# An attention and pooling kernel on one core: head pairs interleaved in the columns of q and k, and the first two batches' score rows sent from SBUF to SBUF

## The reference, cut to what matters

```
query = side + b_self;   q = query @ Wq + bq
k     = (x + b_prev) @ Wk + bk          # keys of the batch's own 256 tokens
k_s   = query @ Wk + bk                 # one more key for each query: its own
v, v_s likewise from x and side, without the biases b_prev, b_self
score = softmax([q.k / 4 with keys >= seq_len masked,  (q * k_s).sum / 4])
x     = x + (score @ [v, v_s]) @ Wo + bo
# second layer
s = tanh(x @ W1 + b1) @ v1;  p = softmax(s under one of three masks, by kind)
out = x + (p @ x) / count
```

## Time and profile before

| | before |
|---|---|
| median of 3 runs | 281.02 us (279.83 to 283.24) |
| profiled execution | 281.62 us |
| its span, first to last instruction | 279.9 us |
| busy: PE / DVE / ACT / POOL | 238.4 / 184.4 / 156.6 / 76.3 us |
| chain that ended last: PE / DVE / DMA / issue | 59 / 13 / 9 / 8 % of the span |
| mean granted TensorE clock | 0.95 of full speed |
| DMA traffic | 35.50 MB in 28021 packets, 24416 of them under 2 KB |

### The profile page before, as it was taken

The page is one execution under the profiler, slowest core; times in us unless marked ns, Lnnn a source line. Parts: engine busy times, 40 slices in busy tenths (PEclk is TensorE's granted clock), DMA queues, the critical chain, the costliest instruction groups (busy, mean ns, idle before and its releaser), DMA issues.

```text
span 279.9 us, 6089 instructions
## 1 busy us (share of the span) xinstructions
PE 238.4 (85%) x2100; PEld 187.4 (67%) x2100; DVE 184.4 (66%) x384; ACT 156.6 (56%) x297; POOL 76.3 (27%) x87
## 2 busy tenths in 40 slices
PE   2986898599979999999999989999999769886732
PEld 2984787367758777877788768777787455563622
DVE  2659655457469758875887588758985885335631
ACT  4351223376477557755785667557856546772430
POOL 8026011013025103610451035103511330316111
PEclk9999669599999999999999999999999997999977
DMA  5469636913865096609560946096409410011011
GB/s 152 103 235 233 138 112 182 210 31 115 242 142 188 5 248 134 228 16 252 119 227 20 256 108 225 18 246 118 150 33 261 95 72 2 8 34 37 0 40 37
DMA packets 28021, 35.50 MB, mean 127 GB/s; under 512 B 4440, under 2 KB 24416, under 8 KB 28000
## 3 DMA queue, kind: packets, MB, share of 16 engines
q1 hardware_dynamic: 27360, 33.12, 44.6%
q0 software_dynamic: 640, 2.10, 2.0%
HBM read 20.26 MB, written 14.69 MB: 125 GB/s over the span
## 4 chain that ended last, share of the span: by engine, by line
PE 59%; DVE 13%; DMA 9%; issue 8%; ACT 5%; SPq 3%; POOL 1%; ACTq 0%; DVEq 0%; POOLq 0%
PE ps_any L1080 20%; PE ps_any L1134 10%; PE ps_max L1108 9%; PE ps_any L1087 6%; DMA k_rows<-k_spill 5%; PE ps_exp L1121 4%; DVE s_max L887 4%; DMA k_spill<-k_lo 3%; PE ps_any L1184 3%; PE ps_any L1240 2%; DVE bv_cast L854 2%; SPq L418 1%; ACT pt L623 1%; PE ps_any L1200 1%; PE ps_any L1166 1%
## 5 line engine op out<-in xcount | busy, mean ns | idle before, releaser
L887 DVE TENSOR_REDUCE s_max<-ps_max 128x4 f32<-128x1024 f32 x64 | 78.1, 1220 | 25.1 <-PE ps_max L1108 25.1
L623 ACT ACTIVATE pt<-ps_exp 128x1024 f32<-128x1024 f32 x64 | 65.6, 1025 | 50.1 <-PE ps_exp L1121 49.5
L1108 PE MATMUL ps_max<-k_rows,q_rows 49*128 49x256 f32 x256 | 33.7, 343 | 13.0 <-DMA k_rows<-k_spill 7.2
L1108 PEld LDWEIGHTS ps_max<-k_rows,q_rows 49*128 49x128 f32 x256 | 20.2, 194 | 24.6 <-DVE s_max L887 10.4
L1134 PE MATMUL ps_any<-pt,v_aug 128*32 128x256 f32 x512 | 36.0, 401 | 0.0
L1121 PE MATMUL ps_exp<-q_rows,k_rows 51*128 51x256 f32 x256 | 27.0, 288 | 2.3 <-ACT pt L623 2.3
L578 POOL TENSOR_TENSOR attn<-num,rden 128x256 f32<-128x256 f32 x16 | 9.6, 621 | 54.0 <-DVE rden L1030 54.0
L1121 PEld LDWEIGHTS ps_exp<-q_rows,k_rows 51*128 51x128 f32 x256 | 20.3, 191 | 4.1 <-ACT pt L623 2.7
L569 POOL TENSOR_TENSOR prod_lo<-prod,prod_hi 128x512 fp32r<-128x512 f32 x8 | 10.3, 1282 | 42.2 <-ACT prod_hi L714 42.2
L1080 PE MATMUL ps_any<-st_hi,w_hi 128*128 128x256 f32 x64 | 20.9, 326 | 0.3 <-DVE st_lo L912 0.3
L1134 PEld LDWEIGHTS ps_any<-pt,v_aug 128*32 128x32 f32 x512 | 13.7, 112 | 10.5 <-issue 1.3
(11 more groups left out here) (145 smaller groups left out, 605.3 us busy)
## 6 DMA issues: line engine op xcount, KB each, us to landing
q_rows<-q_spill SPq DMA_DIRECT2D x32, 192.0 KB, 4.4
k_rows<-k_spill SPq DMA_DIRECT2D x32, 192.0 KB
q_spill<-q_hi SPq DMA_DIRECT2D x16, 256.0 KB, 2.5
k_spill<-k_hi SPq DMA_DIRECT2D x16, 256.0 KB, 2.5
s_sb<-in_fside_BxSxS SPq DMA_DIRECT2D x8, 256.0 KB, 3.7
x_sb<-in_x SPq DMA_DIRECT2D x8, 256.0 KB, 3.2
q_spill<-q_lo SPq DMA_DIRECT2D x8, 256.0 KB, 2.2
k_spill<-k_lo SPq DMA_DIRECT2D x8, 256.0 KB, 3.1
```

What stands on the lines that cost most here:

```text
L623: nc.scalar.activation(pt[:, 2 * j % 8:2 * j % 8 + 2], ps_exp[:], ACT.Exp).then_inc(p_ready, 1)
L887: nc.vector.tensor_reduce(s_max[:, j // MJ, :, :, j % MJ].rearrange("p t e -> p e t"), ps_max[:], AX.X, ALU.max).then_inc(max_found, 1)
L1108: last = pe.matmul(ps_max[:, e, t], q_rows[par][rows, j, P * t:P * t + P], k_rows[par][rows, j, :], start=True, stop=True)
```

## The change

The 256 columns of q and of k are dealt out in another order. Before, block 0 held the first heads of all pairs and block 1 the second ones. Now the first 64 partitions of both blocks hold the first heads and the last 64 the second ones, and the two blocks hold alternate pairs. So 64 partitions by two blocks are, read in order, 16 partitions by 8 pairs, which is the order of the score rows.

With that, the rows of batches 0 and 1 are sent straight from SBUF to SBUF (`direct`): 12 DMAs of 128 KB per batch, each from 64 partitions to 16, in 2 KB pieces; SP issues them, but for the four of k_hi of batch 0, which ACT issues. TensorE's wait at j = 0 is then for all rows of q and k (both halves). Batches 2 to 7 still go through DRAM, with both blocks of a partition side by side there, so that a spill is 128 pieces of 2 KB (before: 256 of 1 KB), and a placing is as large as before. The loads of batch 1 come behind batch 0's rows on SP, no longer before them.

The set-up changes too: bq and bk are loaded by four DMAs (before two); POOL sets the second buffer's ones ahead of its first other work (before: at the end of period -1); ACT's split of Wo moves behind `prod_hi`; in period -1 DVE computes k_lo before the product q * k_s; the output bias (`bias_out`) is added in period 0; the sum over a head's dimensions (`headsum`) and the copy of the own-key scores follow the new order.

```diff
-        q_spill = nc.dram_tensor("q_spill", [2, 3, P, S], F32).ap()
-        k_spill = nc.dram_tensor("k_spill", [2, 3, P, S], F32).ap()
...
+        q_spill = nc.dram_tensor("q_spill", [3, P, 2, S], F32).ap()
+        k_spill = nc.dram_tensor("k_spill", [3, P, 2, S], F32).ap()
...
+        def direct(queue, part, rows, sixteens, sent):
+            for c in sixteens:
+                for e in range(2):
+                    queue.dma_start(rows[64 * e + DH * c:64 * e + DH * c + DH].bitcast(F32),
+                                    part[P // 2 * e:P // 2 * e + P // 2].rearrange("p m t -> p (m t)").bitcast(F32)
+                                    ).then_inc(sent, 16)
+
+        def parts_free(engine, i, k, spilled, direct_sent, sent_per):
+
+            if isinstance(i, int) and 0 < 2 * i + k < 3:
+                engine.wait_ge(direct_sent, sent_per * (2 * i + k))
+            elif (n := count(i, k, 48, -96)) is not None:
+                engine.wait_ge(spilled, n)
...
-                if (n := held(count(i, k, placed_per, 0))) is not None:
+                if (n := held(count(i, k, placed_per, -2 * placed_per))) is not None:
...
-                            sp.dma_start(dram[:, c].rearrange("e p t -> p e t"), parts[part][:].bitcast(F32)
-                                         ).then_inc(spilled, 16)
+                            sp.dma_start(dram[c], parts[part][:].bitcast(F32)).then_inc(spilled, 16)
...
                     sp.dma_start(rows[64 * e:64 * e + ROWS, MJ * g:MJ * g + MJ].bitcast(F32),
-                                 dram[e].rearrange("c (d j) t -> (c d) j t", d=DH)[:, MJ * g:MJ * g + MJ]
+                                 dram.rearrange("c (e d g l) m t -> e g c d (l m t)", e=2, g=NM, l=2)[e, g]
...
+            def direct_q(i, k):
+
+                if i * 2 + k == 0:
+                    sp.wait_ge(rows_one, 2)
+                sp.wait_ge(q_copied, count(i, k, 1, 1))
+                direct(sp, q_hi, q_rows[k % 2], (0, 1), q_direct)
+                sp.wait_ge(q_lo_done, count(i, k, 1, 1))
+                direct(sp, q_lo, q_rows[k % 2], (2,), q_direct)
...
+            def direct_k(i, k):
+
+                if i * 2 + k > 0:
+                    sp.wait_ge(k_hi_done, count(i, k, 1, 1))
+                    direct(sp, k_hi, k_rows[k % 2], (0, 2), k_direct)
+                else:
+                    sp.wait_ge(masks_stored, 16)
+                mask = row(mask_dram, i, k).unsqueeze(0).unsqueeze(0).broadcast_to([2, NJ, S])
+                sp.dma_start(k_rows[k % 2][R_MASK:R_MASK + 65:64].bitcast(F32), mask).then_inc(k_direct, 16)
+                sp.wait_ge(k_lo_done, count(i, k, 1, 1))
+                direct(sp, k_lo, k_rows[k % 2], (1,), k_direct)
...
-                if isinstance(i, int) and 2 * i + k < 2:
+                if isinstance(i, int) and 0 <= 2 * i + k < 2:
                     load(i, k + 2)
...
+                if isinstance(i, int) and 2 * i + k < 1:
+                    direct_q(*nxt)
+                    if live(*b):
+                        place_max(*b, 0)
+                    direct_k(*nxt)
+                    if not live(*b):
+                        load(i, k + 2)
+                    if live(*prv) and not last:
+                        load_again(*prv)
+                    return
...
-                        elif g == 0:
-                            sp.wait_ge(rows_one, par + 1)
...
-                        if g == 0 and isinstance(i, int):
-                            sp.wait_ge(masks_stored, 16)
...
-                    sp.dma_start(bqk_raw[:, n, :], vec.rearrange("(j e d) -> d j e", e=2, d=DH)
-                                 ).then_inc(bias_loaded, 16)
+                    for m in range(2):
+                        sp.dma_start(bqk_raw[:, n, m:m + 1],
+                                     vec.rearrange("(j m f) -> m f j", m=2, j=MJ)[m].unsqueeze(2)
+                                     ).then_inc(bias_loaded, 16)
...
+            ones_rows(1)
...
+                parts_free(pool, i, k, spilled, q_direct, 96)
...
-                if first:
-                    ones_rows(1)
...
-                        dst = dst.rearrange("p (e d j) -> p e d j", e=2, d=DH)
-                        src = src.rearrange("p (j e d) -> p e d j", e=2, d=DH)
+                        dst = dst.rearrange("p (m f j) -> p m f j", m=2, j=MJ)
+                        src = src.rearrange("p (j m f) -> p m f j", m=2, j=MJ)
...
-                            act.wait_ge(k_spilled, n)
+                        parts_free(act, *c, k_spilled, k_direct, 112)
...
                         if first:
-                            weight_hi(3)
+                            act.wait_ge(rows_one, 2)
+                            act.wait_ge(k_hi_done, 1)
+                            direct(act, k_hi, k_rows[0], (0, 2), k_direct)
...
+                        if first:
+                            weight_hi(3)
...
-                        nc.scalar.activation(s_self[:, c[1] % 2].rearrange("p g t e j -> p (g t e j)"),
-                                             ps_any[:, bank_of("SS", *c), 0, 0:2 * H], ACT.Copy
+                        nc.scalar.activation(
+                            s_self[:, c[1] % 2].rearrange("p g t e (l m) -> p (g t) (e l) m", m=2),
+                            ps_any[:, bank_of("SS", *c), 0, 0:2 * H].rearrange("p (b m x) -> p b x m", m=2, x=4), ACT.Copy
...
-                    act.wait_ge(q_spilled, n)
+                parts_free(act, i, k, q_spilled, q_direct, 96)
...
-                dve.wait_ge(bias_loaded, 4 * 16)
+                dve.wait_ge(bias_loaded, 6 * 16)
...
+            def k_low(i, k):
+
+                dve.wait_ge(k_hi_done, count(i, k, 1, 1))
+                parts_free(dve, i, k, k_spilled, k_direct, 112)
+                for m in range(2):
+                    last = nc.vector.scalar_tensor_tensor(
+                        out=k_lo[:, m], in0=ps_any[:, bank_of("K", i, k), m],
+                        scalar=bqk_col[:, 1, m:m + 1], in1=k_hi[:, m].bitcast(F32),
+                        op0=ALU.add, op1=ALU.subtract)
+                last.then_inc(k_lo_done, 1)
...
                         setup_pooling()
+                    if isinstance(i, int) and (2 * i + k, s) == (0, 2):
                         dve.wait_ge(bv_product_ready, 1)
                         nc.vector.tensor_tensor(bias_out[:], bo_wide[:], ps_exp[:, 0, 0], ALU.add
                                                 ).then_inc(bias_out_done, 1)
...
+                            for g in range(NM):
+                                last = nc.vector.tensor_reduce(
+                                    headsum[:, MJ * g:MJ * g + MJ].rearrange("p (e l) -> p e l", e=2),
+                                    ident[:].rearrange("p (e d g l) -> p g e l d", e=2, g=NM, l=2)[:, g],
+                                    AX.X, ALU.max)
+                            last.then_inc(headsum_ready, 1)
...
+                        if first:
+                            k_low(*c)
+                            product(*c)
+                        else:
+                            product(*c)
+                            k_low(*c)
...
                 if j % MJ == 0:
-                    pe.wait_ge(q_placed[j // MJ], count(i, k, 32, 32))
-                    pe.wait_ge(k_placed[j // MJ], count(i, k, 48, 48))
+                    if isinstance(i, int) and 2 * i + k < 2:
+                        pe.wait_ge(q_direct, 96 * (2 * i + k + 1))
+                        pe.wait_ge(k_direct, 112 * (2 * i + k + 1))
+                    else:
+                        pe.wait_ge(q_placed[j // MJ], count(i, k, 32, -32))
+                        pe.wait_ge(k_placed[j // MJ], count(i, k, 48, -48))
...
-                by_block = bank[:, 0, 0:2 * H].rearrange("p (g t e j) -> p t e g j", g=NM, t=KB, e=2)
+                by_block = bank[:, 0, 0:2 * H].rearrange("p (g t m x) -> p t m g x", g=NM, t=KB, m=2)
                 for t in range(KB):
-                    for e in range(2):
+                    for m in range(2):
                         for part in (prod_hi, prod_lo):
-                            last = pe.matmul(by_block[:, t, e], part[:, e, P * t:P * t + P], headsum[:],
+                            last = pe.matmul(by_block[:, t, m], part[:, m, P * t:P * t + P], headsum[:],
```

45 lines of the change are left out of this document (16 added, 29 removed).

## The result

The changed kernel takes **367.84 us** (median of 4 runs, 364.14 to 369.5) against 282.13 for the kernel before on the same chip (4 runs, 279.83 to 285.58): a ratio of 1.306, 95% interval 1.289 to 1.322. It is 30% slower. The prediction was 277.6 in a range of 270 to 285.5. The profiled execution took 366.49 us (span 364.8), 84.9 more than the one before.

A forecast was written before the change was run, and what follows sets the result against it. TensorE was taken to bound itself from period 2 on, with all gains in the first 80 us. Terms 0.9 - 2.4 - 1.5 - 0.4 = -3.4 took 281.62 to 278.2; the median, 0.6 lower, was 277.6, range 270 to 285.5.

The forecast's parts named there:

- slower: Whole kernel: a time above 286.6 us, the worse half of rival B, direct DMAs over 1.32 us each; chance 0.09.
- Term 4: Batch 2's 2.12 us wait: spills ahead of it may run faster with 2 KB pieces; -0.4 us (0 to -1.15).
- Term 1: Start to batch 1's transposes: set-up, direct rows and the load behind them move these from 28.61 to 29.5; +0.9 us.
- The hold: Set-up: POOL's memsets hold DVE's small bias operations to 10.8, so the bias products come 2.1 us late.
- rival B: Direct rows starved by their 16 partitions, 1.26 us per DMA: slower by 4.6 us, a median of 285.6; chance 0.20.
- Term 2: Batch 1's rows: six direct DMAs are there at 49.9 instead of 52.35; -2.4 us (bounds -3.15 and 0).
- Term 3: Clock behind batch 1's wait: the half-clock stretch goes if that wait shrinks to 0.7; -1.5 us (bounds 0 and -4.7).
- Rival C: Nothing won: the start is held as long as the waits shrink; 281 us, within 1.5; chance 0.12.

The follow-up runs named there:

- pad_before: The kernel before with each third of the spilled rows starting 8 DRAM rows further on, so a placing's source no longer merges; 374.49 us, ratio 1.337.
- mended: The changed kernel with DRAM ordered feature, part, pair: spills are one DMA of 128 partitions, a placing's slowest dimension is 16; 280.8 us, ratio 0.996.
- split_before: The kernel before with each of a batch's six spills sent as two DMAs of 64 partitions instead of one of 128; 305.05 us, ratio 1.081.
- two_queues: mended with the direct DMAs of batch 0's high q parts shared between SyncE's queue and ScalarE's, by partition halves; 280.72 us, no ratio given.
- roundtrip: merged with batches 0 and 1 also sent through DRAM and batch 1's loads ahead of the rows again; 303.95 us, ratio 1.083.
- merged: The changed kernel with partition halves outermost in DRAM: a placing reads 48 even rows, a spill is two DMAs of 64 partitions; 305.48 us, ratio 1.086.

## Why the prediction was wrong, step by step

**The step that failed** is the sentence "From period 2 on TensorE bounds itself, and the change leaves that work as it is", with "Later batches wait 0.4 in all" behind it. The bytes and the number of placings stayed, the form of one did not. Its source went from a dimension of 48 rows to 3 by 16, and with that, by the share of 0.19, from 16 DMA engines to 3. I had taken that a placing costs as before because it has as many bytes and rows. `pad_before` alone is 94 us slower. `mended` wins the loss back. Nearly all of the miss is here: 78.7 of the 84.9 us lie behind 63.61, where only rows that go through DRAM are still to come. That a spill has to stay whole as well, I learned from `split_before`. The 0.09 that I gave to "slower" was for direct DMAs of over 1.32 us; they took 1.1 to 1.2, so the 30% does not bear it out. Term 4, for the longer pieces, is not seen: the wait of batch 2 in `mended` is 1.99, against 2.12.

**Term 1** (+0.9 forecast; +7.4 in the trace: batch 1's transposes start at 36.02, not 28.61). The hold came nearly as forecast (2.57 us, products 1.7 late and not 2.1). A direct DMA was mis-sized: 131 thousand bytes at the measured 112 to 121 GB/s are 1.1 to 1.2 us, not 0.84. That is above the 0.97 from which rival B decides, and B's first score at 32.1 was nearer to the 34.10 measured than the forecast's 27.9. B had counted ten of the twelve DMA times; all twelve stood in one line, 19.1 + 12 x 1.17 + 0.4 = 33.5. That is the line which the Trainium skill (DMA: Bandwidth & Descriptors, "Issuing engines are not separate DMA queues") speaks of, and for neighbouring partitions the trace agrees: from 21 us on the rate stays near 120 with ScalarE's DMAs still under way. In `two_queues`, with spread partitions, more than the issue time was won. The Trainium skill's table (SBUF — State Buffer, "Door 1: The DMA port swizzle") has 104 GB/s for 16 neighbouring partitions; the trace is above it by 14% (119 GB/s from 21 to 33 us). I had the rule in hand and gave it 0.20. Batch 1's side input came behind the rows, at 36.02 with a wait of 1.13, as described.

**Term 2** (-2.4). Batch 1 waited 4.72, not less than 3.15: six DMAs issued from 47.94 had landed by 58.5. In `mended`, with rows over 46 partitions, the wait for rows is gone: the mechanism was right, the rate decided it.

**Term 3** (-1.5). The sentence behind it, that both slow stretches follow idle time, does not carry over. In the changed kernel TensorE is at half clock from 26 to 29.3 us, ahead of its wait for batch 0's rows and without a gap. In `mended` it is at half clock from 46 to 54, and that begins before batch 1's first score at 51.78, while TensorE is busy; in `two_queues` the same stretch runs at full clock (us, busy (count), granted clock, DMA share, GB/s; in this order):

```profile
26.00:29.30 3.30, 3.30 (x13) 0.50 1.05 113
```

```profile
46.00:54.00 8.00, 7.01 (x47) 0.50 0.38 123
```

```profile
46.00:54.00 8.00, 5.89 (x62) 1.00 0.32 104
```

So that stretch did not hang on the wait for rows, and the term has no ground; what it hangs on is open. Where the waits were long, in batches 2 to 7 of the changed kernel, the clock was low behind each of them, and no term had that. The other way, the slow stretch behind batch 0's rows was shorter than before: 0.50 from 30 to 40 us there, full clock again from 40 on now, six microseconds behind the first score. From batch 1's transposes to its wait for rows TensorE needed 17.8 us (20.6 before). So its delay of 7.4 us at those transposes was 6.2 at batch 2's, although the wait between them was 1.6 longer.

**The sum without the failed step.** `mended` is the nearest to it: the change with whole spills and placings at the old rate, though with faster direct rows. It gave 0.996 (0.989 to 1.003). The forecast, 277.6 of 281.02, is 0.988, just below that interval, so the forecast gain of 3.4 us is not shown even there. Nor do its pieces fit: a faster rate than in the changed kernel made term 2, and term 3 is missing.

**Rival C**, nothing won (281 within 1.5, or 0.995 to 1.005), describes `mended` better than the forecast does, and I had given it 0.12. That the direct rows decide little is also what `roundtrip` against `merged` shows.

## What to carry to other kernels

When a DRAM layout changes, write down for each DMA that reads or writes it the dimensions that are left after merging, on both sides: the slowest one decides how many DMA engines work, and 3 by 16 is another DMA than 48 with the same bytes. In a trace the sign is a low, flat DMA share (0.19 is three of sixteen) under a long queue, with waits on unrelated loads behind it. When two forms of a spill are possible, keep its SBUF side on all 128 partitions: `merged` mended one side and broke the other, `mended` mended both by swapping the order of feature and part.

## What the runs showed of the hardware

- DMAs that write 16 partitions ran at 108 to 137 GB/s (119 from 21 to 33 us of the changed kernel) when they are neighbours. When they are every third of 46, it was 139 to 180 in most microseconds of `mended` and 131 to 270 with two queues, at a DMA share near 1.0 in all three. The share tells how long the engines are held, not what they move.
- Spills of 64 partitions moved 194 to 210 GB/s, of 128 partitions 309 to 385. With 64 it was the same for pieces of 1 KB (`split_before`) and of 2 KB (`merged`).
- The issue of a DMA of 16x4x512 cost 0.60 to 0.71 us on SyncE and 0.72 on ScalarE, which issued at the same time as SyncE's 0.71. That of a placing cost 0.38 to 0.56 in the kernel before, 0.59 to 0.63 in `mended` (but for one pair of 1.1 each) and 0.69 to 1.39 in the changed kernel.
- A transfer behind narrow ones in the queue waits for them: the reload of x landed after 18.14 us, with the DMA share at 0.24 or less from 130 to 138 us of them.
- TensorE's granted clock was at half from 46 to 54 us in `mended` and at full in the same stretch of `two_queues`, with no wait for rows before batch 1's first score in either.
